# The third tree's up sum in two pieces: 5 units at the end of a slot, 11 behind the next slot's first subtractions

## What is computed

```
x = x + xattn(layernorm(x), ctx)      # 16 heads of 64, softmax over 2048 keys
x = x + retention(layernorm(x))
x = x + forward(layernorm(x))
def fff(x, nw, nb, w1, b1, w2, b2, act):   # a tree of depth 8: 256 leaves
    node = 0
    for _ in range(8):
        node = 2*node + 1 + (x . nw[node] + nb[node] > 0)
    leaf = node - 255
    h = act(x @ w1[leaf] + b1[leaf])       # 16 hidden units of 128 products
    return h @ w2[leaf] + b2[leaf]
def forward(x):
    xn = (x - mean) / sqrt(std + 1e-5)
    q, k, v = fff(xn, q...), fff(xn, k...), fff(xn, v...)   # relu
    y = xn + softmax(q @ k.T / sqrt(128)) @ v
    return y + fff(y, f...)                                  # gelu
```

## Time and profile before

| | |
|---|---|
| median of 3 runs | 648.02 us (645.96 to 648.12) |
| profiled execution | 649.7 us, of it 647.9 us span from the first to the last instruction |
| granted TensorE clock, mean | 0.995 of full speed |
| busy: PE / DVE / ACT / POOL | 616.6 / 471.1 / 393.2 / 263.6 us (95 / 73 / 61 / 41 % of the span) |
| distance of two `neg_max`, slots 33, 34, 35, 36 | 10.03, 9.25, 7.77, 9.26 us |

### The profile page before, as it was taken

How to read it: one execution, slowest core, us unless ns; L and a number is a source line. 1 busy time by engine, 2 the same in 40 slices (tenths; PEclk the granted TensorE clock), 3 DMA queues, 4 the chain that set the end, 5 groups by cost and what they waited for, 6 DMA issues and landing times.

```text
span 647.9 us, 10070 instructions
## 1 busy us (share of the span) xinstructions
PE 616.6 (95%) x3755; PEld 512.9 (79%) x3755; DVE 471.1 (73%) x846; ACT 393.2 (61%) x834; POOL 263.6 (41%) x252
## 2 busy tenths in 40 slices
PE   8899999999999999998999999998999999888887
PEld 5678888888888888877888888777888888875674
DVE  3666657778777777878786877978777877765853
ACT  3765565676665555777654855867565856642571
POOL 2210001130202103997434156997252347964533
PEclk9999999999999999999999999999999999898999
DMA  8910000020100004340030027140030008021933
GB/s 194 245 34 1 1 1 1 0 63 5 66 1 1 1 1 174 162 134 1 1 136 1 0 70 286 50 135 1 1 135 2 2 11 328 1 70 65 342 136 139
DMA packets 21399, 48.49 MB, mean 75 GB/s; under 512 B 1508, under 2 KB 14696, under 8 KB 17256
## 3 DMA queue, kind: packets, MB, share of 16 engines
q0 software_dynamic: 4608, 34.74, 14.4%
q1 hardware_dynamic: 16168, 12.85, 7.4%
q10 hardware_dynamic: 576, 0.26, 0.1%
HBM read 47.59 MB, written 0.26 MB: 74 GB/s over the span
## 4 chain that ended last, share of the span: by engine, by line
PE 66%; POOL 13%; DVE 10%; ACT 5%; DMA 3%; issue 3%; POOLq 0%; DVEq 0%; ACTq 0%
PE ps_s L470 23%; PE ps_av L470 20%; PE ps_ring L745 14%; PE ps_ring L470 5%; PE ps_m L470 4%; POOL leaf L1590 4%; DVE chunk_max L1437 2%; POOL leaf L1594 2%; DMA w_room<-down_v_dram,idx 2%; ACT prob L1095 2%; DVE pt L1180 2%; POOL ct_lo L1559 2%; ACT pt L1023 1%; DVE hid L1249 1%; DVE tree L1271 1%
## 5 line engine op out<-in xcount | busy, mean ns | idle before, releaser
L1023 ACT CAST pt<-ps_ring 128x512 fp32r<-128x512 f32 x256 | 144.5, 590 | 153.3 <-PE ps_ring L745 153.1
L1180 DVE TENSOR_TENSOR pt<-ps_ring,pt 128x512 fp32r<-128x512 f32 x256 | 170.4, 686 | 49.0 <-ACT pt L1023 48.7
L470 PE MATMUL ps_av<-pt,c_hi 128*128 128x512 f32 (+1 forms) x544 | 189.9, 396 | 1.2 <-issue 1.2
L1095 ACT ACTIVATE prob<-ps_s,neg_max 128x1024 f32<-128x1024 f32 x128 | 141.6, 1114 | 23.0 <-DVE neg_max L1524 22.9
L745 PE MATMUL ps_ring<-ident,prob 128*128 128x128 f32 x1024 | 145.0, 274 | 10.6 <-DVE x_sb L1469 4.3
L1437 DVE TENSOR_REDUCE chunk_max<-ps_s 128x1 f32<-128x1024 f32 x128 | 150.6, 1216 | 3.1 <-PE ps_s L470 2.9
L745 PEld LDWEIGHTS ps_ring<-ident,prob 128*128 128x128 f32 x1024 | 117.6, 141 | 37.1 <-issue 24.2
L470 PE MATMUL ps_av<-pt,c_lo 128*128 128x256 f32 x512 | 143.7, 281 | 0.0
L470 PEld LDWEIGHTS ps_av<-pt,c_hi 128*128 128x128 f32 x544 | 101.0, 190 | 21.3 <-issue 2.3
L470 PE MATMUL ps_s<-ct_hi,q_hi 128*128 128x512 f32 x256 | 112.5, 439 | 2.9 <-ACT prob L1095 1.6
L470 PE MATMUL ps_s<-ct_hi,q_lo 128*128 128x512 f32 x256 | 101.6, 397 | 0.0
(11 more groups left out here) (293 smaller groups left out, 723.6 us busy)
## 6 DMA issues: line engine op xcount, KB each, us to landing
stage<-ctx_t_dram SPq DMA_DIRECT2D x16, 256.0 KB, 4.0
stage<-ctx_rows_dram SPq DMA_DIRECT2D x16, 256.0 KB, 3.0
leaf<-w_v_dram SPq DMA_DIRECT2D x1, 512.0 KB, 8.5
leaf<-w_o_dram SPq DMA_DIRECT2D x1, 512.0 KB, 10.8
dec<-decay_dram SPq DMA_DIRECT2D x1, 512.0 KB
nw<-node_w_dram SPq DMA_DIRECT2D x1, 510.0 KB
wsm<-w_small_dram SPq DMA_DIRECT2D x1, 448.0 KB
leaf<-wq_t_dram SPq DMA_DIRECT2D x1, 384.0 KB, 11.5
```

Source lines behind the costliest of these rows:

```text
L470: return nc.tensor.matmul(o, l, r, start=start, stop=stop)
L1023: nc.scalar.copy(pt_hi[:, pp, row:row + KPC, P * (n % 2):P * (n % 2 + 1)], ps_ring[:, i % 2, :].rearrange("p (k q) -> p k q", k=KPC)).then ...
L1095: nc.scalar.activation(prob[:, n % 2, 1024 * e:1024 * (e + 1)], ps_s[:, 1024 * e:1024 * (e + 1)], ACT.Exp, bias=neg_max[:, n:n + 1], accum ...
L1180: return nc.vector.tensor_tensor(o, a, b_, op)
```

## The change

For batches 0 and 1 alone, DVE's `hid2` sums only units 0 to 4 (`FIRST_HID = 5`), at its place at the end of slot 33 (49). A new step `more_hid2` with number 68 sums units 5 to 15 in the middle of slot 34 (50), behind the slot's first two subtractions and ahead of `attmax`, and increments `hid_ready`. ACT's four `down2` instructions, that stood two and two in the quarters 1 and 2, stand together in quarter 2. POOL's and PE's order is as it was.

```diff
 DVE_AT = dict(of="DVE", ...
-              pick_v=58, hid0=61, hid1=62, hid2=67, out0=65, ...
+              pick_v=58, hid0=61, hid1=62, hid2=67, more_hid2=68, out0=65, ...
...
+FIRST_HID = 5
...
                 for g in range(CH):
                     for k, b in steps_at(ACT_AT, s, 0):
-                        if k[:4] == "down" and s < HEADS and g in (1, 2):
+                        if k == "down2" and s < HEADS:
+                            if g == 2:
+                                down_part(b, 2, 0, shares(b, 2)[1])
+                        elif k[:4] == "down" and s < HEADS and g in (1, 2):
...
+            def third_hidden(b, first, end):
+
+                w = up_rows_at(b, 2)[:, D * first:D * end].rearrange("p (l d) -> p l d", d=D)
+                dve.wait_ge(S["up_ready"], 4 * b + 3)
+                return nc.vector.reduce_sum(hid[:, 2, first:end], w, axis=AXX)
...
+                elif k == "hid2" and b < B - 2:
+                    links[0] += 1
+                    third_hidden(b, 0, FIRST_HID).then_inc(S["dve_link"], 1)
+                elif k == "more_hid2":
+                    if b < B - 2:
+                        third_hidden(b, FIRST_HID, LW).then_inc(S["hid_ready"], 1)
```

More of the change, by code:

```diff
@@ L53 @@
 DVE_AT = dict(of="DVE", x1=41, xn1=42, rope=44, silu=45, decay0=46, decay1=47, norm=49, x2=52, xf=53, turns=55, turns_v=57, pick=56,
-              pick_v=58, hid0=61, hid1=62, hid2=67, out0=65, out1=66, attmax=68, y=72, turns_f=73,
+              pick_v=58, hid0=61, hid1=62, hid2=67, more_hid2=68, out0=65, out1=66, attmax=68, y=72, turns_f=73,
               pick_f=74, hid3=81)
@@ L70 @@
     ("PE", "third_sum"): 90,
-    ("DVE", "hid2"): 1000,
+    ("DVE", "hid2"): 1000, ("DVE", "more_hid2"): 1000,
     ("DVE", "out0"): 1000,
@@ L97 @@
     ("ACT", "qk_t"): 65, ("ACT", "att"): 67, ("ACT", "attp_t"): 68, ("ACT", "v_copy"): 69, ("ACT", "gelu"): 80, ("ACT", "down3"): 82, ("ACT", "out_copy"): 83,
-    ("DVE", "out0"): 1000, ("DVE", "out1"): 1000, ("DVE", "hid2"): 65, ("DVE", "attmax"): 66,
+    ("DVE", "out0"): 1000, ("DVE", "out1"): 1000, ("DVE", "hid2"): 65, ("DVE", "more_hid2"): 1000, ("DVE", "attmax"): 66,
     ("Pool", "relu1"): 63,
```

## The result

The changed kernel took 651.25 us (median of 13 runs, 648.67 to 655.65) against 648.3 us of the kernel before (13 runs, 645.96 to 650.51) on the same chip: ratio 1.0057, 95 % interval 1.0039 to 1.0075, or +3.7 us (2.5 to 4.9). The ratio and its interval are formed over all runs and lean to the long ones: five of the 13 took over 653 us, and none of the kernel before. The two medians lie 2.95 us apart. It is slower, by somewhat more than the +2.45 us that was forecast. The profiled execution took 650.24 us, its span 648.4.

What follows compares the result with a forecast made beforehand. POOL's chain to the c_lo splits was taken to bind at slot 35's context half: +1.22 us per batch, +2.44 us over two batches, on 648.0 us gives 650.5 us (+0.4 %), range 648.6 to 652.3.

Steps and rivals of the forecast that it cites:

- The first wait: PE's idle time ahead of slot 34's second transposes shrinks from 1.70 to 0.25 us.
- The two pieces: DVE's sum cut into five and eleven units takes 0.82 and 1.61 us, 0.16 more than whole.
- DVE gains nothing: In slot 34 DVE does the same work between the same neighbours; attmax starts at 301.57 instead of 301.50.
- PE's lead is lost: PE's 1.45 us lead falls to 0.5 at slot 34's attention transpose, then becomes 0.66 us of lateness.
- ACT 0.66 us late, hidden under POOL's lateness: Two unit products moved behind att delay ACT's exponentials and PE's next transposes by 0.66 us; POOL's lateness hides this.
- POOL decides: Later hid_ready delays POOL's fold, c_lo splits and slot 35's context half by 1.22 us per batch.
- POOL does not bind: Rival, chance 0.15: the wait ahead of the context half is not POOL's; only ACT's 0.66 us per batch count, 649.3 us.
- the lead survives: Rival, chance 0.09: attention and query cast have unseen slack, PE keeps 1.45 us per batch, 645.1 us.
- The two delays: Rival, chance 0.20: ACT's and POOL's lateness add up at POOL's fold, 1.88 us per batch, 651.8 us.
- The sum: Both batches together: +1.22 us per batch, +2.44 us in all, added to the runs' median of 648.0 us.
- the rival that I had named for it: The two delays adding up at POOL's fold, chance 0.20: slower by over 0.5 %, 651.8 us.

Runs made afterwards that it cites:

- ACT's part: Kernel before, with only ACT's four third tree products together in quarter 2 and DVE's sum whole where it was; ratio 1.0010 to the kernel before.
- the splits moved ahead: Changed kernel and kernel before, each with fold2 and out2 on POOL behind the context's first two splits; ratios 0.9992 and 0.9991 to the kernel before.
- eleven and five: Changed kernel with 11 units in the first piece and 5 in the second (FIRST_HID = 11); ratio 1.0044 to the kernel before.
- the repetition: Changed kernel measured once more, unaltered; ratio 1.0057 to the kernel before.

## Why the prediction was right, and where it was short

**The first wait.** Forecast to shrink from 1.70 to 0.25 us; it has 0.23.

**The two pieces.** Forecast 0.82 and 1.61 us; they take 0.80 and 1.61. The sizes by the table of the Trainium skill, "VectorE: DVE Perf Modes", section "The TRN2 errata — SBUF-src ops pay a fixed extra latency per instruction", 0.73 and 1.53, are too short here. The section itself says behind the table that this row under-predicts the duration of a single instruction, which the prediction did not take in. Its warning against cutting is a matter of 0.14 us here (0.80 + 1.61 - 2.27).

**DVE gains nothing.** `attmax` was to start at 301.57; it starts at 301.55 on that scale.

**PE's lead is lost.** Forecast waits of 0.9 ahead of the attention's transpose and about 1.1 ahead of slot 35's second transposes; 0.87 and 0.94 were found; the second falls some 0.2 us short, about what a bracket leaves out. Those transposes start at 307.28 + 1.12 = 308.40, forecast 308.41.

**ACT 0.66 us late, hidden under POOL's lateness.** The exponentials are 0.65 us late. Alone, ACT's part costs 0.55 to 0.57 us a batch, nearly the whole pair of products (0.59). With POOL's chain out of the way in both kernels the change costs 0.64.

**POOL decides.** The fold was to start at 304.92 and does at 303.77 + 1.12 = 304.89; the context half at 313.15, found at 313.08. The step is 1.15 us, forecast 1.22. The sum of the two is +2.3 us where I had +2.44.

**The rivals.** That POOL does not bind fell with the splits moved ahead. That the lead survives fell in the changed kernel's own profile, and the kernel with eleven and five shows that the size of the lead is without effect. The two delays did not add up: 1.15 us per batch, not 1.88.

**What fell short: the step from the trace to the time.** The sum took it that the runs shift by what the slots shift. By the ratios they shifted by +3.7 us (2.5 to 4.9), in the repetition by +3.7 (2.2 to 5.3), and with eleven and five by +2.9 (1.6 to 4.1). The steps are +2.3 in each, below the first interval and in the lower part of the other two. By the medians the three differences are 2.95, 2.56 and 2.33 us, so most of the excess is in a part of the runs: five of 13 and three of 12 took over 653 us, and no run of the kernel before took 651. The one of these that was profiled has its excess ahead of slot 33 and behind slot 52. Whether the change makes such runs more frequent, and how, or whether this is scatter between measurements, stays open. A lower mean clock goes with it, but does not settle it: at equal clocks the repetition has a difference of 2.4 us (0.992), while with eleven and five the medians differ by 0.7 us at 0.992 (two runs against six) and 3.7 us at 0.995 (five against four). The mechanism of the two stretches is as forecast. That the ratio came out on the far side of 0.5 %, at 1.0057 with an interval that holds both sides, is not due to the rival that I had named for it.

## What to carry to other kernels

A stall of one engine is worth only what the neighbours let through. Before moving work out of it, walk the new order through every engine to the next point where they meet; here the same DVE work stood between the same two neighbours, and the maxima did not come earlier. Ask who waits for the result of the moved work: a sum that ends 2.82 us later (298.91 + 1.61 + 1.12 = 301.64, against 298.82) delays the engine that consumes it, and everything queued behind, though the producer has lost next to nothing. Move work into an idle time of its own engine (0.84 us on DVE), rather than out of the idle time of another, and look for unrelated work (the splits) that stands behind a late chain for no reason but the order.

## What the runs showed that I had not expected

A wait of TensorE can be longer than its bracket. The idle time is counted from the modelled end of the product before, although the next would have started some 0.2 us ahead of it. Removing a wait shown as 0.60 us (0.61 in batch 1) brought 0.84 and 0.85 us.

After an idle time of 2.03 to 2.06 us TensorE went on at 1.2 GHz for 3.4 us at one of four places. After idle times of at most 1.14 us, in 12 places of six profiles, it never did. But the length of a single wait does not decide it. In the repetition the clock was at 1.2 GHz from 34.25 to 37.70 us, and the waits just before were these:

```profile
32.13 0.50 PE L471 MATMUL ps_s<-ct_hi,q_hi 128*128 128x512 f32 x1 [0.52 <-ACT prob L1096]
...
34.03 0.88 PE L746 MATMUL ps_ring<-ident,prob 128*128 128x128 f32 x4 [0.94 <-DVE q_lo L1184]
```
